# A gated group convolution on one core: the 3x3 conv on eight array tiles, column sums by folds, gate products on two engines

## The reference

```python
ch = conv1x1(concat[mean(gx), max(gx)], w_cc, b_cc)            # per channel
channel_weight = sigmoid(gn(ch, gn1_w, gn1_b))
hw = conv1x1(concat[row means, column means], w_s1, b_s1)
pos_h = sigmoid(conv1x1(hw rows, w_ph, b_ph))                   # one value a row
pos_w = sigmoid(conv1x1(hw columns, w_pw, b_pw))                # one value a column
sx = conv3x3(gx * pos_h * pos_w, w_s3) + b_s3                   # 16 -> 16 channels, 'SAME'
spatial_weight = sigmoid(gn(sx, gn2_w, gn2_b))
out = x + gx * channel_weight * spatial_weight
```

## Time and profile before

| what | value |
|---|---|
| median of three runs | 4297.4 us (4295.71 to 4300.11) |
| profiled execution: its own time, its span | 4296.2 us, 4294.3 us |
| granted TensorE clock, mean over the span | 0.965 |
| busy share of PE, DVE, ACT, POOL | 94%, 94%, 61%, 41% |
| time of DMA packets, share of 16 engines | 74.7% |

### The profile page before, as it was taken

One profiled execution on the slowest core, in us unless ns is written; L12 is line 12 of the kernel. 1 busy time (PEld: TensorE's weight loads), 2 busy tenths in 40 slices (PEclk: granted clock), 3 DMA queues, 4 the chain that ended last, 5 costly groups with the idle time before them and its releaser, 6 DMA issues.

```text
span 4294.3 us, 55492 instructions
## 1 busy us (share of the span) xinstructions
PE 4041.4 (94%) x11016; PEld 1938.2 (45%) x11016; DVE 4018.4 (94%) x2719; ACT 2624.4 (61%) x4354; POOL 1775.4 (41%) x2314
## 2 busy tenths in 40 slices
PE   5999999999999999999999999999999999999997
PEld 2444444444444444444444444444444444444443
DVE  7999999999999999999999999999999999999996
ACT  3566566666665666666656666666666666665665
POOL 3443444444434434443344434344444344434443
PEclk9999999999999999999999999999999999999998
DMA  6777777777777777777777777777777777777775
GB/s 124 163 173 173 172 175 169 175 172 173 172 173 169 177 173 172 175 167 178 172 172 172 172 176 172 171 172 176 168 177 173 172 175 167 177 173 173 171 177 123
DMA packets 1147751, 730.57 MB, mean 170 GB/s; under 512 B 74144, under 2 KB 1122976, under 8 KB 1147552
## 3 DMA queue, kind: packets, MB, share of 16 engines
q1 hardware_dynamic: 1147552, 728.87, 74.7%
HBM read 268.64 MB, written 268.44 MB: 125 GB/s over the span
## 4 chain that ended last, share of the span: by engine, by line
DVE 53%; issue 18%; SPq 11%; DMA 9%; PE 6%; POOL 1%; ACT 1%; DVEq 1%; POOLq 0%; ACTq 0%
DVE sums L560 13%; DVE mx L607 12%; SPq L222 11%; DMA xt<-in_x 9%; DVE sp_buf L524 7%; DVE sums L554 7%; DVE gated L567 7%; DVE sp_buf L527 6%; PE conv_ps L637 5%; POOL rstd L275 1%; ACT sp_buf L416 1%; DVE gate_hr L594 0%; PE pos_ps L637 0%; DVE ch L603 0%; DVE sums_n L545 0%
## 5 line engine op out<-in xcount | busy, mean ns | idle before, releaser
L637 PE MATMUL conv_ps<-gated,W_conv 128*128 128x512 f32 x6144 | 2973.1, 619 | 16.5 <-DVE gated L567 16.3
L637 PEld LDWEIGHTS conv_ps<-gated,W_conv 128*128 128x128 f32 x6144 | 1143.4, 197 | 1100.0 <-issue 1071.7
L637 PE MATMUL conv_ps<-halo,W_halo 96*128 96x512 f32 x2048 | 1027.7, 604 | 2.1 <-DMA halo<-gated 1.6
L370 ACT ACTIVATE sp_buf<-conv_ps,weights 128x1024 f32<-128x1024 f32 x512 | 565.3, 1104 | 747.8 <-PE conv_ps L637 747.5
L323 POOL TENSOR_TENSOR gated<-gate_w,gate_hr 128x2048 f32<-128x2048 f32 x256 | 918.7, 3609 | 166.9 <-DVE gate_hr L594 157.6
L560 DVE TENSOR_REDUCE sums<-xt 128x128 f32<-128x2048 f32 x256 | 943.6, 3725 | 0.0
L554 DVE TENSOR_REDUCE sums<-xt 128x16 f32<-128x2048 f32 x256 | 584.2, 2282 | 171.5 <-DMA xt<-in_x 171.4
L524 DVE SCALAR_TENSOR_TENSOR sp_buf<-xt,negm,sp_buf 128x2048 f32<-128x2048 f32 x256 | 600.6, 2346 | 38.3 <-ACT sp_buf L416 38.3
L527 DVE SCALAR_TENSOR_TENSOR sp_buf<-sp_buf,kfac,xt 128x2048 f32<-128x2048 f32 x256 | 602.1, 2352 | 9.0
L567 DVE SCALAR_TENSOR_TENSOR gated<-xt,negm,gated 128x2048 f32<-128x2048 f32 x256 | 593.9, 2361 | 0.0
L343 POOL TENSOR_TENSOR rstd<-var_e,consts 128x2 f32<-128x2 f32 x128 | 89.8, 701 | 1176.8 <-DVE var_e L581 1176.8
(11 more groups left out here) (79 smaller groups left out, 2174.4 us busy)
## 6 DMA issues: line engine op xcount, KB each, us to landing
xt<-in_x SPq DMA_DIRECT2D x2048, 128.0 KB, 3.0
out<-sp_buf SPq DMA_DIRECT2D x2048, 128.0 KB, 2.5
halo<-gated SPq DMA_DIRECT2D x512, 365.2 KB, 6.0
weights<-in_by_channel SPq DMA_DIRECT2D x1, 116.5 KB, 2.6
S_chan<-in_same_channel SPq DMA_DIRECT2D x1, 64.0 KB, 1.9
whalo_in<-in_wconv SPq DMA_DIRECT2D x2, 3.0 KB, 1.8
masks<-in_row_masks SPq DMA_DIRECT2D x1, 12.0 KB, 1.9
hmask<-in_halo_mask SPq DMA_DIRECT2D x1, 3.0 KB, 1.9
```

What stands on the lines that cost most here:

```text
L370: nc.scalar.activation(sp_buf[:, g, k * 8:k * 8 + 8], conv_ps[:, h % 2], ACT.Identity, bias=V["b_s3"], accum_out=ssum2[:, g, k:k + 1]).the ...
L637: return nc.tensor.matmul(ps, lhsT, rhs, start=start, stop=stop)
```

## The change

1. **Layout.** Partition `32*(r//2) + 2c + r%2` now holds row residue r of channel c. So 32 consecutive partitions hold two row residues of all 16 channels. The conv's weights get wrap-around masks, and the tables for the weights come expanded from the host.
2. **Conv.** Instead of 128x128 matmuls and a halo matmul, `tiles` issues matmuls of 64 rows x 32 columns. The output columns of pair `o` (32 partitions) take their input from the upper or the lower 64 partitions. The neighbouring block of rows is reached by an offset of one block in `gated`, which now has one zero block on each side. A `slot` issues, for each of three taps, four tiles of the upper half into bank n and four of the lower half into bank n-1 (of the slot before), so eight positions of the array are addressed. That makes 8 slots x 3 taps x 8 = 192 matmuls a unit. PE waits on its own semaphore `upper_mm` before the lower half writes to a bank.
3. **Halo** buffer, its weights and its 4 DMAs a unit are gone.
4. **Column sums** become two adds (`fold8`: 8x128 elements, `fold4`: 4x128) a group; the last four rows are summed by four accumulating matmuls in `positions`. `sums_n` is gone: the mean enters `positions` by two more matmuls.
5. **Gate products**: POOL makes that of half 0, ACT that of half 1, by 16 activations of 128 elements.
6. **Evacuation** in 8 pieces of 512 columns instead of 4 of 1024. The order of the small matmuls and of ACT's queue changes with it.

```diff
 # DVE
-                    for j in range(2):
-                        nc.vector.tensor_scalar(sums_n[:, da, j, 0:NB], sums[:, da, j, 0:NB], 1.0 / W,
...
                 def column_sums(j):
-                        nc.vector.tensor_reduce(sums[:, dc, j, NB:], xt[:, sc, j].rearrange("p b w -> p w b"), AX_X,
-                                                ALU.add).then_inc(sums_done, 1)
+                        n = 2 * c + j
+                        if later(n, 1):
+                            dve.wait_ge(fold4_done, n)
+                        nc.vector.tensor_tensor(fold8[:], xt[:, sc, j, 0:8], xt[:, sc, j, 8:16],
+                                                ALU.add).then_inc(fold8_done, 1)
+                        dve.wait_ge(fold8_done, n + 1)
+                        if later(c, 2):
+                            dve.wait_ge(pos_mm, c - 1)
+                        nc.vector.tensor_tensor(fold4[:, dc, j], fold8[:, 0:4], fold8[:, 4:8],
+                                                ALU.add).then_inc(fold4_done, 1)
 # ACT, body
                 if real(b):
-                    evacuate(b, sb_, 3)
+                    evacuate(b, sb_, 7)
...
+                if real(t):
+                    evacuate(t, q, 0)
+                    evacuate(t, q, 1)
                 if real(b):
                     square2(b, sb_, 1)
...
+                if real(t):
+                    evacuate(t, q, 2)
                 if real(b):
                     variance2(b, sb_, 1)
                 if real(t):
-                    evacuate(t, q, 1)
+                    evacuate(t, q, 3)
+                if real(a):
+                    act.wait_ge(ghr_done, a + 1)
+                    act.wait_ge(gates_done, 4 * a + 4)
+                    if later(a, 2):
+                        act.wait_ge(conv_mm, 8 * (a - 2) + 8)
+                    for i in range(NB):
+                        ins = nc.scalar.activation(gated[:, da, 1, 1 + i, 1:1 + W], gate_w[:, da, 1], ACT.Copy,
+                                                   scale=gate_hr[:, da, 1, i:i + 1])
+                    ins.then_inc(gp_act, 1)
                 if real(b):
                     spatial_gate(b, sb_, 1)
                 if real(t):
+                    evacuate(t, q, 4)
                     square2(t, q, 0)
...
+                    evacuate(t, q, 5)
                     variance2(t, q, 0)
                     spatial_gate(t, q, 0)
+                    evacuate(t, q, 6)
 # PE
+                        mm(pos[:, :, 0:NB], W_rows[:, :], sums[:, da], stop=False)
+                        mm(pos[:, :, 0:NB], W_rows_m[:, :], shift.to_broadcast([P, 2, NB]), start=False)
+                        for i in range(4):
+                            mm(pos[:, :, NB:NB + W], W_cols[:, :], fold4[:, da, :, i], start=i == 0, stop=False)
+                        mm(pos[:, :, NB:NB + W], W_cols_m[:, :], shift.to_broadcast([P, 2, W]),
+                           start=False).then_inc(pos_mm, 1)
+                def tiles(u, d, n, half, kw, start):
+
+                    j, k = n // BANKS, n % BANKS
+                    for o in range(PAIRS):
+                        band = 1 + BB * k
+                        if half == 1 and o == 0:
+                            band -= 1
+                        if half == 0 and o == PAIRS - 1:
+                            band += 1
+                        rows = slice(ROW_TILE * half, ROW_TILE * (half + 1))
+                        cols = slice(QUAD * o, QUAD * (o + 1))
+                        ins = mm(conv_ps[cols, k], W_conv[rows, kw, cols],
+                                 gated[rows, d, j, band:band + BB, kw:kw + W], start=start and kw == 0,
+                                 stop=not start and kw == KW - 1)
+                    return ins
+
+                def slot(n, first=0, last=KW):
+
+                    if real(t) and first == 0:
+                        if n % BANKS == 0:
+                            pe.wait_ge(mod_done, 2 * t + n // BANKS + 1)
+                        if later(8 * t + n, BANKS):
+                            pe.wait_ge(evac, 8 * t + n - BANKS + 1)
+                        pe.sem_inc(bank_free, 1)
+                    for kw in range(first, last):
+                        if real(t):
+                            ins = tiles(t, q % 2, n, 0, kw, True)
+                            if kw == KW - 1:
+                                ins.then_inc(upper_mm, 1)
+                        if real(t) if n > 0 else real(b):
+                            if kw == 0:
+                                pe.wait_ge(upper_mm, 8 * t + n)
+                                pe.sem_inc(upper_ready, 1)
+                            if n > 0:
+                                ins = tiles(t, q % 2, n - 1, 1, kw, False)
+                            else:
+                                ins = tiles(b, sb_ % 2, 7, 1, kw, False)
+                            if kw == KW - 1:
+                                ins.then_inc(conv_mm, 1)
 
                 mean()
...
                 maxima()
...
+                slot(0)
+                slot(1)
                 mean2(b, sb_, 1)
...
+                positions()
+                slot(2)
+                slot(3, 0, 1)
                 variance()
...
+                channel()
+                slot(3, 1, KW)
+                slot(4)
                 var2(b, sb_, 1)
...
+                slot(5)
                 mean2(t, q, 0)
...
+                slot(6)
+                slot(7)
                 var2(t, q, 0)
```

More of the change, by code:

```diff
@@ L23, with conv_attention @@
 KW = 3
-HALO = 2 * CG * KW
-HALF = 2
 BB = 4
-RUN = (NB - 2) * WP + W
-W_LOADS = 6
+BANKS = NB // BB
+PAIRS = RB // 2
+QUAD = 2 * CG
+ROW_TILE = P // 2
+W_LOADS = 3
 PER = 4
-def conv_attention(nc, x, by_channel, wconv, same_channel, row_masks, halo_mask, out):
+def conv_attention(nc, x, by_channel, same_channel, row_masks, out):
     x_g = x.rearrange("n (g c) (b r) w -> (n g) r c b w", c=CG, r=RB)
@@ L73, in conv_attention @@
         S_chan = sb("S_chan", [P, P])
-        sums = sb("sums", [P, 2, 2, NB + W])
-        sums_n = sb("sums_n", [P, 2, 2, NB + W])
+        sums = sb("sums", [P, 2, 2, NB])
+        fold8 = sb("fold8", [P, 8, W])
+        fold4 = sb("fold4", [P, 2, 2, 4, W])
+        W_rows_m = sb("W_rows_m", [P, P])
+        W_cols_m = sb("W_cols_m", [P, P])
         tot = sb("tot", [P, 2, 2])
@@ L118, in conv_attention @@
         x_in = [[sem(f"x_in{s}{j}") for j in range(2)] for s in range(XS)]
-        halo_in = [[sem(f"halo_in{s}{j}") for j in range(2)] for s in range(2)]
         stored = [sem(f"stored{s}") for s in range(4)]
@@ L138, in conv_attention @@
         evac = sem("evac")
+        bank_free = sem("bank_free")
+        upper_mm = sem("upper_mm")
+        upper_ready = sem("upper_ready")
         mean2_mm = sem("mean2_mm")
@@ L382, in square2 @@
                     act.wait_ge(sig2, n - 3)
[L384 removed]
+                nc.scalar.activation(share2[:, g], gn2_ps[:, 0:BANKS], ACT.Copy, scale=-1.0,
                                      accum_out=negm2[:, g:g + 1]).then_inc(negm2_done, 1)
                 act.wait_ge(negm2_done, n + 1)
[L387 removed]
+                act.wait_ge(evac, BANKS * (n + 1))
                 if later(n, 1):
```

208 lines of the change are left out of this document (70 added, 138 removed).

## The result

The changed kernel takes 4938.2 us (median of four runs, 4937.4 to 4949.3) where the kernel before took 4296.6 in the same session: ratio 1.150, 95% interval 1.148 to 1.152. It is 15% slower, outside the predicted range. The forecast's loop from PE to ACT and back is there, but TensorE walks a good part of it at half clock, and POOL's queue, which the forecast did not follow to its end, makes a second loop of nearly the same length.

What follows compares the result with a forecast made beforehand. DVE was taken to bound the kernel before, the way from PE to ACT and back afterwards: 4294.3 + 127 x (32.4 - 33.05) + 5 = 4217 us, so 4220 us median, 1.8% less; range 3910 to 4480 us, this case 4050 to 4340.

Steps and rivals of the forecast that it cites:

- loop from PE to ACT and back: Way from PE's body through ACT's queue back to PE, said to set the period at 32.4 us a unit.
- the walk of the queues: Step timing PE's and ACT's instructions in order from the start of PE's body; next body starts at 32.4 us.
- S to the end of `var2(b, 1)`: PE's leg from the start of its body (S) until `var2(b, 1)` is done, put at 20.7 us.
- The clock takes it back: Rival: TensorE's clock falls after stops, costing about 1.7 us of matmul; 34.1 us a unit, 4435 us; chance 0.24.
- The argument against it: Point against the clock falling: PE's wait is slack, and a slowdown in slots 5 to 7 falls into it.
- three changes at 0.6 us: Three changes between tiles and whole array on PE before S + 20.7, each uncertain by +-0.6 us.
- The rival of serial tiles: Rival: PE's tiles do not run side by side, 0.43 us a matmul, 91 us a unit, 11.7 ms; chance 0.10.
- The stop at `channel`: PE stands still 1.9 us at `channel`, waiting for POOL's `gmx_n`, with the conv's slot 3 behind it.
- The end of `var2(b, 1)` to `var2(t, 0)` by ACT: ACT's leg from `variance2` through evacuations, gate product and `spatial_gate(b, 1)` to `square2(t, 0)`: sum 11.5 us.
- DVE's share of 75%: Sign that the forecast is right: DVE's busy share falls to 85% or less, with 27.5 us of work a unit.
- Looser loop: Rival: mode changes cost nothing, lower tiles don't lag, `channel`'s wait hides; 30 us a unit, 3912 us; chance 0.22.
- DVE stays the bound by POOL's lock: Rival: POOL's product locks out DVE's folds, up to 3.6 us; 32.5 us a unit, 4230 us; chance 0.05.

Runs made afterwards that it cites:

- p1: Changed kernel with POOL's gate product ahead of `rstd2_power(b, 1)`: 4798.2 us, ratio 1.117 to the kernel before.
- f3: Changed kernel with `channel` behind the rest of slot 3, ACT's product ahead of evacuation 2, `channel_norm` ahead of `rstd2_power(b, 1)` and POOL's product: 4373.7 us.
- f1: Changed kernel with POOL's `channel_norm` ahead of `rstd2_power(b, 1)` and the gate product: 4876.8 us, ratio 1.135 to the kernel before.
- h2: Changed kernel with only the eight-tile convolution: both gate products on POOL, column sums by strided reduce with `sums_n`: 5605.3 us, ratio 1.305 to the kernel before.
- k1: j1 with POOL's product and `channel_norm` beside one-input DVE passes, `mx` ahead of the folds, `kfac` and `cgate` reordered: 4039.6 us, ratio 0.941 to the kernel before.
- g1: Kernel before with the folds for the column sums alone, both gate products on POOL: 4626.6 us, ratio 1.078.
- e1: Changed kernel with `channel` moved behind the rest of slot 3: 4521.2 us, ratio 1.052 to the kernel before.
- e2: Changed kernel with ACT's product loop ahead of evacuation 2 in place of behind evacuation 3: 5107.6 us, ratio 1.189 to the kernel before.
- j1: f3 with PE's queue written out for 20 units a turn, not 4: 4211.7 us, ratio 0.982 to the kernel before.
- f4: Changed kernel with PE's two stops filled with matmuls nobody reads and `channel_norm` early: 4534.1 us, ratio 1.056 to the kernel before.

## Why the prediction was wrong

**The step that failed** is the walk of the queues, in two places.

- *Its PE legs were at full clock.* S to the end of `var2(b, 1)` was put at 20.7 us; it ends at 25.4 (2500.82 to 2525.84, and 0.38). Of these 4.7 us the clock has 4.3: 8.13 us for slots 0 and 1 where the full clock gives 5.74 (2.4); 6.38 for 80 passes where p1's trace, at full clock there, has 4.88 (1.5); and about 0.4 in `mean` and `maxima` (0.96 us, 0.53 at full clock in f3). The rival "The clock takes it back" was the right mechanism at the wrong size: it counted one slow stretch of 1.7 us. There were two on the loop, one behind each stop, and they cost 3.9 us of conv. The argument against it, that a slowdown falls into PE's slack, was wrong: each stop lies just ahead of the stretch that is on the loop. With 4.3 in place of 1.7 the walk gives 32.4 + 4.3 + 0.6 (0.4 more in this leg, and 0.44 us from `var2(t, 0)` to the next body where it had 0.2) = 37.3 us, and a unit without the jump lasts 37.36 (2500.82 to 2538.18).
- *It stopped at POOL's product.* It said that the product would come at about 21 "when DVE is at the maxima, a reduce". It came at 26.4 and reached past the maxima, so that `maxima_in` behind them took 2.12 us, and what stands behind it in the queue, `channel_norm` and `rstd2_power(t, 0)`, was not walked. That loop alone costs less in the changed kernel (61 us back by f1, 140 by p1), but it hides what a cure of the clock gives (99 us with it, 343 without), and with both products on POOL it is 752 of the 1310 us that h2 loses.

**Missed altogether**: PE's jump back. The waits give `PE norm_ps` with nothing to wait for 99.2 us in 29 times, 3.4 us each; eight tiles made the queue nearly five times as long (53256 matmuls, 11016 before). That the length is the reason is my reading; the runs show that the stop is at the jump.

**The range.** The bounds that the prediction names, three changes at 0.6 us and ACT's product at 4.6 or 5.6, add up to 2.0 us below and 2.6 above the 32.4: about 3,970 to 4,550 us, and not 4,050 to 4,340. It was too narrow by its own terms, and the measured time lies outside either.

**Terms that held.** The tiles run side by side: a slot of 48 passes takes 2.73 us at full clock (2526.16 to 2528.89), against the forecast's 2.57, so the conv's own time is 21.8 us and not 20.6. The rival of serial tiles is dead; the Trainium skill, page "TensorE: Matmul & The Clock Gate", section "Part 3: Packing small matmuls", has starts and ends strictly in program order, and if both passes of a tile stand next to each other in the queue, each tile's second pass would by that have held up the next tile. The times do not show it: 48 passes in 2.73 us are 0.455 us for eight. In which order the passes stand in the queue no trace here tells. Folds: 1.22 and 0.72 us against 1.25 and 0.70, as long as no product lies beside them. ACT's product: 4.78 us (k1: 4.81) against 4.8. The stop at `channel`: 1.79 against 1.9. The end of `var2(b, 1)` to `var2(t, 0)` by ACT: 11.5 (2526.22 to 2537.74) against 11.5. ACT's work: 26.1 us a unit (3346.2 / 128) against 26.2; its share is 68% and not 80, because the period grew. For the same reason DVE's share of 75%, which looks like a hit, is no support: its work is 29.1 us a unit (3725.7 / 128) and not 27.5.

**Rivals.** "Looser loop" is what k1 approaches (30.6 us a unit), with TensorE's stops nearly gone. "DVE stays the bound by POOL's lock" holds in g1, not in the changed kernel, whose folds run free because the product is late.

## What to carry to other kernels

Where an engine's stop lies just ahead of the part that closes the loop, price the stop together with the slow clock behind it: here a stop of 1.8 us was worth 3.3 us a unit (e1). Follow a strict queue past the instruction that you moved, to its last one, and note for each what the other engine does at that time; one small operation that waited at a queue's head cost 752 us in h2. When two loops are nearly equal, one cure shows little, so cure both before a theory is dropped. Look for a price at a loop's jump as well: writing TensorE's loop out for 20 units gave 73 and 162 us.

## What the runs showed of the hardware

- A stop's length alone does not tell what the clock does after it. 80 passes took 6.38 us behind a stop of 1.79 in the changed kernel and 6.41 behind one of 1.61 in e2, but 4.88, full clock, behind one of 1.61 in p1, and 6.35 again behind one of 1.76 in the unit before. In f3 the 96 passes behind a stop of 2.34 took 5.74 us, and the next 96, behind one of 0.97, took 7.43. What decides between them is open.
- POOL operations of 0.20 us took 2.2 us beside DVE's two-input passes, and DVE's `maxima_in`, 0.18 us alone, took 2.7 beside a POOL product in f3 and up to 3.6 in the changed kernel. The reduces (one input) took no such delay in any trace here: the longest full row sum took 2.29 us where the median is 2.28, and a POOL product beside the maxima reduce took its 3.61 us in k1.
- TensorE's jump back cost nothing that the waits name in the kernel before (11016 matmuls), and 3.4 to 3.9 us a jump in the changed kernel, f3 and j1 (53256); in h2 (51976) the waits name 2.0 us a jump.
- One of five executions of f4, the one that was profiled, took 14757 us with a mean clock of 0.34; the other four took 4531 to 4534 us. Around 3000 us its rows show a clock of 0.26, below the lower level, and 96 passes take 19.95 us in place of 5.74. Up to 1300 us the clock is shown as 1.00, yet 96 passes take 31.8 us, so the shown clock does not account for the time there. What put it there is open.
